# VectorE order in the short experts: next pair's k side and first maxima, then the divisions

## The reference

```python
h = _ln(xf, ln1_w, ln1_b)
qkv = h @ ipw.T + ipb
q, k, v = jnp.split(qkv, 3, axis=-1)              # 8 heads of 64
scores = jnp.einsum('htd,hsd->hts', q, k) / jnp.sqrt(D)
scores = jnp.where(mask[None, None, :], scores, NEG)
a = jax.nn.softmax(scores, axis=-1)
o = jnp.einsum('hts,hsd->htd', a, v).transpose(1, 0, 2).reshape(T, E)
o = o @ opw.T + opb
x1 = xf + o                                        # then a two-layer MLP with gelu
```

## Time and profile before

| | us |
|---|---|
| median of 3 runs | 1327.05 |
| lowest and highest of them | 1324.7 and 1328.79 |
| the profiled execution, its own time | 1324.23 |
| the profiled execution, its span | 1322.5 |
| TensorE busy | 1046.1 (79%) |
| VectorE busy | 741.1 (56%) |
| ScalarE busy | 455.0 (34%) |
| GpSimd busy | 322.1 (24%) |
| mean granted TensorE clock | 0.897 |

### The profile page before, as it was taken

One profiled execution on the slowest core, in us unless ns is written; L12 is line 12 of the kernel. 1 busy time (PEld: TensorE's weight loads), 2 busy tenths in 40 slices (PEclk: granted clock), 3 DMA queues, 4 the chain that ended last, 5 costly groups with the idle time before them and its releaser, 6 DMA issues.

```text
span 1322.5 us, 19279 instructions
## 1 busy us (share of the span) xinstructions
PE 1046.1 (79%) x5070; PEld 576.6 (44%) x5071; DVE 741.1 (56%) x1573; ACT 455.0 (34%) x843; POOL 322.1 (24%) x298
## 2 busy tenths in 40 slices
PE   1986799998800888778876959979799899989984
PEld 1654467777800333434333424434344344533333
DVE  5395435441461478736784473674856636736854
ACT  1301121221312366225635314434435451235522
POOL 3102324441367144203441020000000124213311
PEclk9987799998555998989897889999999999989998
DMA  5291000000427115121323020000000312120010
GB/s 148 66 285 50 1 2 0 0 0 1 157 60 233 75 48 164 42 78 32 128 85 120 1 63 1 1 0 0 0 0 3 110 48 75 41 70 1 1 31 33
DMA packets 32650, 74.58 MB, mean 56 GB/s; under 512 B 6253, under 2 KB 6551, under 8 KB 32297
## 3 DMA queue, kind: packets, MB, share of 16 engines
q1 hardware_dynamic: 24269, 55.97, 13.6%
q0 software_dynamic: 8000, 15.44, 4.0%
q10 hardware_dynamic: 288, 2.10, 0.4%
HBM read 50.63 MB, written 24.13 MB: 57 GB/s over the span
## 4 chain that ended last, share of the span: by engine, by line
PE 63%; DVE 16%; issue 10%; ACT 5%; POOL 3%; DMA 1%; DVEq 1%; SPq 0%; ACTq 0%; POOLq 0%
PE bank L1334 16%; PE bank L1425 9%; PE bank L1207 8%; PE bank L1246 5%; PE bank L1455 3%; DVE den L2159 3%; PE bank L1510 3%; PE bank L1242 2%; PE bank L1410 2%; PE bank L1389 2%; PE bank L1412 2%; PE bank L1173 2%; POOL lists L658 1%; PE bank L1469 1%; PE bank L1229 1%
## 5 line engine op out<-in xcount | busy, mean ns | idle before, releaser
L1425 PE MATMUL bank<-probs_t,v_head 128*128 128x512 f32 (+1 forms) x288 | 146.9, 593 | 17.0 <-ACT probs_t L991 16.4
L1789 DVE TENSOR_SCALAR oh_src<-iota,edge 125x1250 f16 x178 | 101.2, 568 | 105.4 <-PE bank L1207 100.5
L2072 DVE TENSOR_REDUCE mx<-bank 128x1 f32<-128x512 f32 x144 | 88.2, 656 | 75.7 <-PE bank L1389 74.9
L991 ACT ACTIVATE probs_t<-bank 128x512 f32<-128x512 f32 x144 | 81.6, 574 | 142.3 <-PE bank L1412 130.1
L560 POOL TENSOR_TENSOR w<-w_stage,w 128x1024 f16<-128x1024 f32 x40 | 85.8, 2158 | 145.9 <-ACT w L804 145.8
L1207 PE MATMUL bank<-oh_src,oh_dst 125*125 x534 | 110.8, 357 | 2.8 <-issue 0.4
L1510 PE MATMUL bank<-probs_t,v_head 128*128 128x128 f32 (+2 forms) x192 | 88.8, 549 | 6.9 <-ACT probs_t L1042 5.1
L1334 PE MATMUL bank<-hT,w 128*128 128x256 f16 (+1 forms) x552 | 89.5, 326 | 1.9 <-DVE hT L2005 1.9
L1207 PEld LDWEIGHTS bank<-oh_src,oh_dst 125*125 x534 | 70.2, 142 | 43.5 <-issue 24.2
L1455 PE MATMUL bank<-hT,w 128*128 128x512 f16 x288 | 72.7, 385 | 7.8 <-ACT t L1016 7.8
L1334 PE MATMUL bank<-w,hT 128*128 128x512 f16 x264 | 68.0, 415 | 10.3 <-DVE hT L2005 10.3
(11 more groups left out here) (306 smaller groups left out, 1956.3 us busy)
## 6 DMA issues: line engine op xcount, KB each, us to landing
w_stage<-in_ew_dram SPq DMA_DIRECT2D x40, 512.0 KB, 3.6
lists<-zeros SPq DMA_DIRECT2D x1, 10340.0 KB, 50.2
x_in<-lists SPq DMA_DIRECT2D x20, 517.0 KB, 6.7
x_mem<-lists SPq DMA_DIRECT2D x3, 1024.0 KB, 6.2
x_mem<-lists SPq DMA_DIRECT2D x1, 2560.0 KB, 10.8
out_dram<-x_mem SPq DMA_DIRECT2D x10, 250.0 KB
big<-in_x_dram SPq DMA_DIRECT2D x10, 224.0 KB
x_mem<-in_x_dram SPq DMA_DIRECT2D x1, 2240.0 KB
```

The lines of the kernel that those rows point to most:

```text
L991: nc.scalar.activation(probs_t[:, x % NPB, 0:cn], stb[x % 2][:, 0:cn], ACT.Exp).then_inc(s_exp, 1)
L1425: nc.tensor.matmul(pvb[(hd * nq + s) % 2][:, 0:cn], v_head[:, hd, kt, :], probs_t[:, (hd * nx + i) % NPB, 0:cn], start=(k == 0), stop=(k = ...
L1789: nc.vector.tensor_scalar(oh_src[:, bass.ds(slot, 1), i, 0:N].rearrange("p a n -> p (a n)"), iota[:, :], edge[:, 0, i, bass.ds(g, 1)], Non ...
L2072: nc.vector.tensor_reduce(mx[:, hd, t, s:s + 1], sbk[i % 2][:, 0:cn], AX.X, ALU.max).then_inc(s_mx, 1)
```

## The change

In `short_pair(j)` the divisions of pair j - 1 stood right behind `maxima_of(2j + 1)`. They now stand behind the block for the next pair, that is behind `split_of(j + 1, 1)`, `second_of(j + 1)` and `maxima_of(2j + 2)`, and ahead of `split_of(j + 2, 0)`. For j = 0 there are no divisions and for j = 3 there is no next pair, so j = 1 and j = 2 alone change: two places in an expert, six in the three short experts. No instruction is added or removed, and the other engines' programs are the same.

```diff
                     maxima_of(2 * j + 1)
-                    if j > 0:
-                        for s in range(nq):
-                            divide_of(j - 1, s)
                     if j < 3:
                         split_of(j + 1, 1)
                         second_of(j + 1)
                         maxima_of(2 * j + 2)
+                    if j > 0:
+                        for s in range(nq):
+                            divide_of(j - 1, s)
                     if j < 2:
                         split_of(j + 2, 0)
```

## The result

| | before | after |
|---|---|---|
| median, us | 1325.88 (4 runs) | 1342.20 (4 runs) |
| lowest and highest | 1322.36 and 1328.79 | 1340.84 and 1343.44 |
| profiled execution, its own time | 1324.23 | 1342.51 |
| its span | 1322.5 | 1340.8 |

The changed kernel takes 1.0128 times as long, with a 95% interval of 1.0109 to 1.0147: about 16 us slower. The forecast was 1337 us and slower; the time lies inside the range, near its upper end. Each ratio of an experiment is taken on one chip.

The account below looks back on a forecast made before the run. TensorE, 63% of the chain, sets the pace and VectorE makes it wait. Added 29.7 less removed 18.8 gives +10.9 us on 1324.23, 1335.1 us; with the runs' median 2.8 us higher, 1337 us was taken, range 1323 to 1343.

Parts of the forecast that it names:

- Removed side: Heads 3 and 5 of the short experts: waits for the k side and slow clock go, 18.8 us removed.
- Expert 1's 1.9 us: Head 3 of expert 1: falls from 9.28 to 7.39 us, 1.9 us removed.
- Added side: Heads 4 and 6, short experts: moved divisions delay the next first reduction, TensorE waits; 29.7 us added.
- The 3.9: Head 6 in experts 0 and 1: a wait of 3.9 us at score tile 2, taken between 2.7 and 4.4.
- three operations held by the two blocks: Head 6 in experts 0 and 1: GpSimd's blocks hold three division operations, making the wait 4.4 us.
- the slow clock in expert 3: Expert 3: half of a clock loss, 0.9 us, in head 4 and none in head 6.
- 0.4 us of it, once: Head 6 of expert 3: 0.4 us for the second bank, on top of a wait of 1.8 us.
- Rival 1: Whole kernel: the waits move and the clock holds, -1.5 to +4 us, 1323 to 1331 us; chance 23%.
- Rival 2: Heads 4 and 6: moved divisions are covered, a real gain of -4 to -10, 1315 to 1322 us; chance 12%.
- rival 3: Heads 4 and 6: ScalarE's k-side copy holds the first score, old waits partly stay; +16 to +24 us; chance 8%.

Follow-up runs that it names:

- the first experiment: Only pair 0's divisions moved, behind the maxima of head 4, pair 1's left in place, against the kernel before: 1328.50 us, ratio 1.0028.

## Why the prediction was right

Changes in the profiled executions, after against before, by the prediction's terms, in us:

| | expert 0 | expert 1 | expert 3 | sum | forecast |
|---|---|---|---|---|---|
| head 3 | -5.4 | -1.8 | -1.8 | -9.0 | -9.1 |
| head 4 | +6.2 | +6.6 | +5.7 | +18.5 | +16.9 |
| head 5 | -3.9 | -4.3 | -0.6 | -8.8 | -9.7 |
| head 6 | +6.2 | +6.4 | +3.9 | +16.5 | +12.8 |
| head 2, head 7, end | +0.7 | -2.0 | 0.0 | -1.3 | 0 |
| all | +3.8 | +4.9 | +7.2 | +15.9 | +10.9 |

- **Removed side, right in size, part of its cause left out.** Head 3 fell to 7.4 and 9.2 us, as said, and its wait went with the divisions. Head 5 gave back 0.9 us less than taken. But in head 3 a weight block of GpSimd held one VectorE operation ahead of `k_both` in each expert, by 1.7 to 2.0 us, and I counted that on the added side alone. In expert 0 it was the last of the divisions (2.36 us), in expert 1 a copy of the k side, in expert 3 its subtraction:

```profile
628.16 2.12 DVE L2119 COPY k_both<-halves 64x512 f16<-64x512 f16 x1
...
1228.32 2.64 DVE L2117 TENSOR_TENSOR halves<-t,halves 128x512 f16<-128x512 f32 x1
```

  TensorE's waits there were 1.66 and 1.65 us, no more than these holds, so by this arithmetic the divisions alone would not have made them. No run takes the block out of head 3 and leaves the divisions, so it is argued, not shown.
- **Expert 1's 1.9 us were a matter of its head 2.** That head ran in part at half clock in the trace of before (11.24 us), which gave VectorE time. In the run with pair 1's move alone it took 9.55 us, and head 3, with the same work, waited 3.49 us instead of 1.66. In the changed kernel the slow clock fell on head 2 of expert 0 instead: head 2 changed by +1.5 and -1.7 us in experts 0 and 1, with no change in it.
- **Added side, mechanism and waits right.** The chain in head 4 (maxima, divisions, side, first reduction) is what happened. Taken as 4.4 and 3.6 us, the waits were 4.10 and 3.47; in head 6, taken as 3.9 and 1.8, they were 4.08 and 1.66. The side's 1.4 us and GpSimd's share were each confirmed by a run of their own. The 3.9 was in part luck: I had three operations held by the two blocks, and one was, the multiplication, while the two behind it took their 0.42 and 0.62 us. The held operation that I read as ending when the block ended did so 0.4 us later (484.37 against 483.95).
- **Mis-sized: the slow clock in expert 3, and what comes with a wait at full clock.** The run with useless matmuls tells the two apart. In experts 0 and 1 the clock took 1.6 and 2.0 us in head 4 and 1.75 and 1.65 in head 6, where I had 1.8 and 1.4. In expert 3 I took 0.9 and none, as its head 3 had kept its clock with 1.8 us lost; it was 1.7 in head 4 and about as much in head 6 (an estimate: the head grew by 3.9 us, of which tile 2 comes 1.8 us later than before and what follows tile 3 another 0.4). That head shows clock 0.84 behind waits of 0.57, 1.66 and 0.21 us one after the other. Together the clock took about 10.4 us and not 7.3. The other part is small and at full clock: with the clock at 1.00 head 4 of expert 0 was 4.6 us longer than before behind a wait of 4.1, and in the five heads the growth at full clock was 0.3 to 0.6 us more than the wait, since tile 3 waits for its bank too. I had 0.4 us of it, once; over all, waits and this, it makes 2 us. Clock 3, this 2 and head 5's 1 us, less the 1.3 us of the row below them, are about the 5 us by which the sum was low.
- **Rival 1** (the waits move, the clock holds, -1.5 to +4) is what that same run is: 1330 us. It did not happen by itself. **Rival 2** fell with the first stretch of head 4; **rival 3** with head 3, which kept no wait.
- **What the prediction did not see** is that the two moves are not independent. The sum was over both, so its total was not hurt, but it credited head 5's saving to the second move. My own expectation of the first experiment was 6 us too high by it.
- The remaining 2.4 us between the two profiled executions lie in stages that the change doesn't touch, 1.9 of them between experts 1 and 3. I take them for scatter; runs of the kernel before span 1322 to 1329 us.

## What to carry to other kernels

When a block of work is moved off one wait, compute at the new place how long after its start the next thing is due that stands behind it, with everything in between, and compare with the old place's slack. Here pair 0's 6 us of divisions had 4.4 us of cover in the old place of expert 0 (from the end of the maxima at 476.6 to the k side at 484.3, less the wait of 3.33) and 2.3 in the new (491.9 - 487.8, less 1.4 for the side and 0.4 for the reduction). Pair 1's had about 3.5 (503.2 - 497.2, less 2.52) and 3.7 (512.6 - 508.4, less 0.4), nearly the same: what made that place dearer in experts 0 and 1 was GpSimd's blocks, 1.95 us of the wait, and in expert 3 it was dearer because the old place had cost only 0.6 us there. The two rows of the old place of pair 0:

```profile
476.35 0.22 DVE L2149 TENSOR_REDUCE neg_max<-mx 128x1 f16<-128x1 f32 x2
...
484.29 0.68 DVE L2117 TENSOR_TENSOR halves<-t,halves 128x512 f16<-128x512 f32 x1
```

A block that fits no gap whole may fit two in parts: with the reciprocals in one and the rest in the other it gave 0.7% where moving the whole lost 1.3%, and 1.5% together with the unhurried side behind the hurried maxima and the owners' operations in an earlier gap. And a wait costs more than its length if it drops TensorE's clock, so count both.

## What the runs showed of the hardware that I had not expected

- 14 useless matmuls in each of six waits made the changed kernel faster, from a ratio of 1.0128 to 1.0020, with the clock at 1.00 in the heads of expert 0 where it had been 0.88 and 0.73.
- Whether a wait drops the clock is not a matter of its length alone. In head 2 a wait of 1.53 us left the clock at full speed in expert 0 of the kernel before and slowed it in expert 1 (9.57 and 11.24 us), and in the kernel after it was the other way round (11.05 and 9.56 us). A wait of 2.69 us in head 4 was followed by a head of 10.72 us in expert 0 and of 12.34 in expert 1, in one execution, and waits of 3.48 and 3.49 us in head 3 by a clock of 0.75 and of 1.00 in another. What decides it the runs don't show.
- A weight block of GpSimd held the copy, subtraction, multiplication or addition of VectorE that came under it, 2.0 to 2.6 us instead of 0.3 to 0.7 where that came early in the block, and reciprocals and reductions never in these traces. Each better order of VectorE's work moved another such operation under a block, which took back a part of the gain.
